# Two tables of partial sums in place of three in a fused attention and expert layer

## The reference

```python
x = _layernorm(x + _L0_attn_ref(x), axis=-1)      # 16 heads of 8: softmax of centred scores, times x
x = _layernorm(x + _L0_ffn_ref(x, ...), axis=-1)  # 64 experts, each token goes to 8 of them
...
xe = jnp.zeros((E, CAP, H)).at[sorted_e, pos].set(tok_sorted, mode='drop')     # at most 128 tokens each
h = jax.nn.silu(jnp.einsum('ech,efh->ecf', xe, w1)) * jnp.einsum('ech,efh->ecf', xe, w3)
ye = jnp.einsum('ecf,ehf->ech', h, w2)
...
out = jax.ops.segment_sum(vals * flat_w[:, None], flat_t, num_segments=T)      # sum over a token's experts
shared = jax.nn.silu(x @ shared_gate.T) * (x @ shared_up.T) @ shared_down.T
```

## Time and profile before

| what | value |
|---|---|
| median of 3 runs | 586.57 us (585.08 to 588.45) |
| the profiled execution | 590.31 us, span 588.5 us |
| busy in the span: PE, DVE, ACT, POOL | 382.1, 328.3, 364.8, 380.9 us |
| granted clock of PE, mean of the span | 0.821 |
| the 64 adds on POOL | 99.2 us busy, first starts at 434.49, last at 554.00 us |
| the 24 loads of the last stage on SP | issued from 553.60 to 572.7 us |

### The profile page before, as it was taken

How to read it: one execution, slowest core, us unless ns; L and a number is a source line. 1 busy time by engine, 2 the same in 40 slices (tenths; PEclk the granted TensorE clock), 3 DMA queues, 4 the chain that set the end, 5 groups by cost and what they waited for, 6 DMA issues and landing times.

```text
span 588.5 us, 8660 instructions
## 1 busy us (share of the span) xinstructions
PE 382.1 (65%) x2956; PEld 163.7 (28%) x2956; DVE 328.3 (56%) x1115; ACT 364.8 (62%) x486; POOL 380.9 (65%) x405
## 2 busy tenths in 40 slices
PE   3799998998997988988988985300238455520000
PEld 3233233333332332333332222100226344320000
DVE  6532868778688688687694483810116333330085
ACT  2699989989988988988989992100115222210046
POOL 3400002777777777777777777777787788888644
PEclk9699999999999999999999997555558755755555
DMA  3699931101001001000000000000138655333596
GB/s 96 187 232 297 378 135 38 55 28 44 10 0 31 5 2 27 3 19 10 1 19 8 2 20 4 11 10 2 33 102 180 115 89 64 36 37 36 103 315 184
DMA packets 73300, 43.66 MB, mean 74 GB/s; under 512 B 13351, under 2 KB 72499, under 8 KB 72864
## 3 DMA queue, kind: packets, MB, share of 16 engines
q1 hardware_dynamic: 51744, 36.18, 21.6%
q0 software_dynamic: 21504, 6.81, 9.9%
HBM read 21.27 MB, written 44.40 MB: 112 GB/s over the span
## 4 chain that ended last, share of the span: by engine, by line
POOL 25%; PE 21%; DVE 20%; issue 13%; ACT 12%; DMA 7%; ACTq 0%; DVEq 0%; POOLq 0%; SPq 0%
POOL records L539 15%; POOL sums L557 9%; ACT large L928 8%; PE PV L712 7%; PE S L696 5%; DMA sums<-centred,target 5%; PE M L614 3%; DVE LR L1188 2%; ACT OT L915 1%; PE M L643 1%; DVE last_stats L1530 1%; PE S L614 1%; DMA records<-rec,index 1%; PE M L637 1%; DVE left L1285 1%
## 5 line engine op out<-in xcount | busy, mean ns | idle before, releaser
L539 POOL DMA_INDIRECT records<-rec,index x256 | 255.4, 998 | 153.7 <-DVE index L1331 76.3
L928 ACT ACTIVATE large<-S,shift 128x1024 f32<-128x1024 f32 x256 | 273.4, 1123 | 24.2 <-PE S L696 22.0
L712 PE MATMUL PV<-large,V 128*9 128x512 f32 x1024 | 135.4, 601 | 0.0
L557 POOL DMA_INDIRECT sums<-centred,target x64 | 99.2, 1550 | 22.1 <-issue 18.5
L696 PE MATMUL S<-LR 64*128 64x512 bf16 x512 | 100.7, 392 | 13.6 <-ACT large L928 9.4
L696 PEld LDWEIGHTS S<-LR 64*128 64x128 bf16 x512 | 24.6, 93 | 155.5 <-ACT large L928 99.2
L980 ACT COPY AK<-S 128x512 f32<-128x512 f32 (+1 forms) x17 | 9.5, 561 | 90.3 <-PE S L815 90.1
L1188 DVE COPY LR<-M 128x1024 bf16<-128x1024 bf16 x49 | 33.4, 681 | 17.0 <-PE M L614 17.0
L815 PE MATMUL S<-ident,X 128*128 128x128 f32 x64 | 15.6, 386 | 41.9 <-DMA X<-records 41.9
L1495 DVE CAST target<-number 128x4 uint32<-128x4 f32 (+1 forms) x17 | 3.0, 179 | 56.5 <-DMA sums<-centred,target 49.3
L1015 ACT ACTIVATE last_log<-last_moments,eps 128x4 f32<-128x4 f32 x8 | 2.4, 295 | 44.8 <-DVE last_moments L1533 44.8
(11 more groups left out here) (176 smaller groups left out, 624.0 us busy)
## 6 DMA issues: line engine op xcount, KB each, us to landing
records<-blank SPq DMA_DIRECT2D x1, 6176.0 KB, 29.9
large<-sums SPq DMA_DIRECT2D x24, 256.0 KB, 4.6
X<-records SPq DMA_DIRECT2D x15, 386.0 KB, 4.1
sums<-blank SPq DMA_DIRECT2D x2, 2112.0 KB
large<-L_ffn_w_dram SPq DMA_DIRECT2D x2, 2048.0 KB, 10.9
records<-rec,index POOLq DMA_INDIRECT x256, 2.1
X<-L_attn_x_dram SPq DMA_DIRECT2D x8, 256.0 KB, 2.8
w2s<-L_ffn_w_dram SPq DMA_DIRECT2D x1, 2048.0 KB, 17.7
```

Source lines behind the costliest of these rows:

```text
L539: pool.indirect_dma_start(records, bass.IndirectOffsetOnAxis(ap=index[:, i * TOP + k:i * TOP + k + 1], axis=0), rec[:, i, :], None, bounds ...
L557: pool.indirect_dma_start(sums[n % SUMS], bass.IndirectOffsetOnAxis(ap=target[:, u, i:i + 1], axis=0), ye[:, u, i, :], None, bounds_check= ...
L712: mm = pe.matmul(PV[g % 2][32 * i:32 * i + VCOLS, :], V[:, b % 2, 2 * c + k, QUAD * g + i, :], E[:, u % 2, i, k, :], start=c == 0 and k == ...
L928: nc.scalar.activation(E[:, u % 2, 2 * (i // 2):2 * (i // 2) + 2, i % 2, :], S[:, 2 * (n % 2):2 * (n % 2) + 2, :], ACT.Exp, bias=shift[:, ...
```

## The change

`SUMS` becomes 2. Add n goes to table n mod 2 and waits for the landing of add n-2. One table fewer is filled with zeros at the start (the first of the two DMAs at `L433` goes), and SP loads 16 parts in place of 24, table 0 first and table 1 second. `last_half` and its semaphore `halves` are gone; `last_sum` adds table 1 to table 0. The table with the last add (63) is now table 1; before it was table 0. `large`, where the parts go, is laid out for two parts a batch by the same formula.

```diff
-SUMS = 3
+SUMS = 2
...
-        halves = sem("halves")
...
-            for j in (1, 2, 0):
+            for j in (0, 1):
                 sp.wait_ge(added[j], 16 * adds_before(j, STEPS))
                 for q in range(EARLY_SUMS):
                     load_part(q, j, others_loaded[q] if j > 0 else base_loaded[q])
             for q in range(EARLY_SUMS, BATCHES):
-                for j in (1, 2, 0):
+                for j in (0, 1):
                     load_part(q, j, others_loaded[q] if j > 0 else base_loaded[q])
...
-            def last_half(q):
-
-                wait(dve, others_loaded[q], 16 * (SUMS - 1))
-                v.tensor_tensor(part(q, 2), part(q, 2), part(q, 1), ALU.add).then_inc(halves, 1)
-
             def last_sum(q, u):
 
                 t = Steps(dve, summed, SUM_STEPS, q * len(SUM_STEPS))
                 wait(dve, base_loaded[q], 16)
-                wait(dve, halves, q + 1)
-                t.step("y", v.tensor_tensor(part(q, 0), part(q, 0), part(q, 2), ALU.add))
+                wait(dve, others_loaded[q], 16)
+                t.step("y", v.tensor_tensor(part(q, 0), part(q, 0), part(q, 1), ALU.add))
...
-            for q in range(EARLY_SUMS):
-                last_half(q)
             for q in range(BATCHES):
-                if q >= EARLY_SUMS:
-                    last_half(q)
                 last_sum(q, q % 2)
```

## The result

The changed kernel takes 600.26 us (median of 4 runs, 599.32 to 601.13), the kernel before beside it 586.42. The ratio is 1.0233, with a 95% interval of 1.0198 to 1.0267: the change costs 11.6 to 15.7 us. The prediction was 601.1.

The account below looks back on a forecast made before the run. POOL leads the chain with 25% of the span, its adds starting one every 1.853 us. Adds 17.7, less 1.6 and 1.6 in the last stage, give +14.5 on 586.57: 601.1 us; own range 596 to 606, overall 591 to 608.

Parts of the forecast that it names:

- adds, early part: POOL's adds 0 to 16, beside SP's record loads: waiting for late landings with two tables costs about 9.5 us.
- adds, quiet part: POOL's last 47 adds: 0.132 us more each, 6.2 us, plus 2.0 for two late landings.
- start of the last stage: From the last add to DVE's first sum: 6.8 us in place of 8.45, a gain of 1.6.
- the last stage's pace: Seven batches of the last stage: ACT becomes the bound at 2.19 us each, a gain of 1.6 us.
- The wake: Time from a landing to the start of the POOL add waiting for it: 0.72 us, against 0.27 for scatters.
- The rival of 0.27: Adds start 0.27 us after a landing, as scatters do; the kernel takes 591.8 us; chance 0.13.
- The rival of 1.0: Adds start 1.0 us after a landing, as the add at 443.77 may show; +22.9, 609.4 us; chance 0.07.
- The walk of the prediction: Add-by-add reckoning of POOL's starts from earlier landings plus 0.72 us; gave 9.2 us for even adds through 16.
- the rival "faster": Two adds in flight shorten early landings to 3.3 us, starts follow by 0.27, no add late; 583.4 us; chance 0.05.
- a rule of the Trainium skill: About 2.0 us fixed cost per GpSimd-issued DMA; by it the adds' change would cost 7 us more than the sum.

Follow-up runs that it names:

- two_swapped: Changed kernel (two tables) with POOL's two waits for an add in turned order, landing first, weighted rows second; ratio 1.0027 to the kernel before.
- three_adds_two_sums: Kernel before, adds still to three tables, but the last stage loads and adds only two (table 1 left out of the result); ratio 0.9894 to the kernel before.
- three_one_wait: Kernel before (three tables), POOL waiting for the weighted rows once a step, at its first add; ratio 0.9983 to the kernel before.
- three_swapped: Kernel before (three tables) with POOL's two waits for an add in turned order; ratio 0.9993 to the kernel before.
- two_adds_three_sums: Changed kernel's adds to two tables, but the last stage still loads and adds three (the third holds zeros); ratio 1.0269 to the kernel before.
- two_one_wait: Changed kernel (two tables), POOL waiting for the weighted rows once a step, at its first add; ratio 1.0143 to the kernel before.
- two_swapped_few_loads: Two tables, POOL's two waits turned, SP loading records at most two steps ahead of PE, not up to four; ratio 1.0009 to the kernel before.

## Why the prediction was right

The time was 600.3 where 601.1 was said, by the mechanism that was named. That the two numbers lie so close is partly luck, as the terms show:

| term | predicted, us | in the traces, us |
|---|---|---|
| adds, early part (0 to 16) | +9.5 | +5.7 |
| adds, quiet part (16 to 63) | +8.2 | +9.9 |
| start of the last stage | -1.6 | -0.9 |
| the last stage's pace | -1.6 | -3.1 |
| sum | +14.5 | +11.6 (by the medians 13.8, 11.6 to 15.7) |

- **The wake.** Two rows gave 0.72; it is 0.74. That an add behind a separate wait starts later than a scatter that holds its wait was inferred from the count of wait instructions, and `two_swapped` shows it. This choice decided the outcome: with 0.27 the kernel is within 0.5% of the one before. The rival of 0.27 gave 591.8; `two_swapped`, which is that rival as a kernel, stands 1.6 us (0.1 to 3.1) above the kernel before, where the rival had 5.2. Its early part was over-sized in the same way (+6.5 said, +3.3 in its trace). The rival of 1.0 rested on a true row: in the raw events add 1 of the kernel before landed at 442.73 and add 4 started 1.04 later. It is an exception of this one place; the same add of `three_adds_two_sums` shows 1.04 again.
- **The quiet part.** 3.25 + 0.74 for two adds gives 6.7 more than before over 47 adds. The walk of the prediction made with this trace's own landings (add 18 at 4.0, add 25 at 3.8, add 26 at 4.3) gives 1.8 on top; predicted were 2.0. The last 1.4 are six adds (25, 42, 43, 47, 59, 60) that start 0.83 to 1.5 after their landing; the row of add 25 at 490.56, idle 0.81, is one. That wasn't foreseen.
- **The early part** is the term that was over-sized, 9.5 against 5.7. The step that failed is the walk that gave each add "the landing that an add issued at about that time had before". Add 4 landed in 3.3 us and add 6 in 4.0, where the walk used 5.2 and 4.5. These landings differ from one execution to the next, with three tables too (adds 4 to 6 of `three_one_wait` landed in 3.2, 4.1 and 3.2), and one trace was taken for the rule. But the difference also goes with the tables. The mean landing of adds 2 to 16, from the raw events, is 4.44, 4.26, 4.03 and 4.22 us in the four kernels with three tables and all loads (the kernel before, `three_adds_two_sums`, `three_one_wait`, `three_swapped`), and 3.74, 3.61, 3.84 and 3.81 in the four with two (the changed kernel, `two_adds_three_sums`, `two_swapped`, `two_one_wait`). Half a us less in each of the walk's eight landings is about the 3.8 us that are missing. So early landings did shrink, as the rival "faster" had it, though not to 3.3; why wasn't tried: it can be the fewer adds in flight, or that the adds come later beside the loads.
- **The start of the last stage.** The last add's landing did fall, to 3.35 (said: 3.8), but the load behind it was held at 2.98 and took 4.12. What was issued just before this load had been changed, and the term took its time over unchanged.
- **The pace.** ACT is the bound, as said, but with 2.06 us for a batch and not 2.19. The 2.19 was ACT's first full turn, from the first operation of batch 1 to that of batch 2; the changed kernel shows 2.18 there (579.89 to 582.07) and 2.06 from then on.

The errors of the terms (-3.8, +1.7, +0.7, -1.5) partly cancel, to -2.9 us. The medians differ by 2.2 us more than the two traces do from the first add on, and no term of the sum accounts for that; this is what brings the total within 0.8 us. By the traces alone the forecast was 2.9 us too high, still slower and well inside its range.

The prediction also weighed a rule of the Trainium skill. The page "DMA: Bandwidth & Descriptors", section "Anatomy of one DMA — SWDGE (gpsimd) path", gives about 2.0 us of fixed cost for setup and completion together. The prediction's estimate put these 2.0 us behind 1.55 us of issue, so setup is counted twice in it. The traces have 3.25 us from start to landing in the middle of the quiet part, with two tables as with three. That is more than the page's figure, and the 1.7 us behind the issue are less.

## What to carry to other kernels

How deep a chain of dependent DMAs must be is a sum: landing plus wake, divided by the engine's step; here 4.0 by 1.85 is 2.2, so two tables were just too few and three enough. The wake counts in this sum, and it depends on how the wait is attached: put the wait that comes last in time where the instruction itself holds it (here: written first), and look in the trace for separate wait instructions. The other wait then has the longer wake, as add 6 of `three_swapped` shows. Where work removed at the end and a wait added in the middle are in one change, cost them apart: the end gave 4.0 us for eight batches, the wait took 0.25 us for each of 62 adds.

## What the runs showed of the hardware

- An indirect DMA on POOL started 0.27 us after what it waited for when it held the wait itself, and 0.74 us after it when the wait was a separate instruction before it. All kernels of this study in which an add waits show it, but for the few adds of the next point. It holds for landings (0.27 in `two_swapped`, 0.74 in the changed kernel) and for DVE's signal (0.27 in the kernel before, 0.74 in `three_swapped`, at add 6).
- In the changed kernel six adds took 0.83 to 1.5 us. The same six (25, 42, 43, 47, 59 and 60) did so in `two_adds_three_sums`, with the same values within 0.01, so it hangs on the place in the program. With turned waits adds 25, 42 and 59 of `two_swapped_few_loads` took 0.45 in place of 0.27, as did add 43 of `two_one_wait`, whose add 60, behind a separate wait, took 1.50. With three tables the slack hides nearly all; the 2.09 us of idle time before add 4 hold one, of 1.04. The cause wasn't tried.
- Most landings took 3.1 to 3.4 us when little else ran (the quiet part, 3.25 in the middle), and up to 6.7 beside SP's loads of 386 KB (add 2 of `three_swapped`).
